# Layer 1 of a graph kernel: a third edge group per turn picked by column copies, the turned one-hot in straight order, and the steps of the engines re-ordered

## What is computed

```python
e_in = jnp.concatenate([x[src], x[dst]], axis=-1)
edge_new = relu(e_in @ We1 + be1) @ We2 + be2
agg = segment_sum(edge_new, dst, num_segments=N)
mesh_new = relu(concatenate([x, agg]) @ Wn1 + bn1) @ Wn2 + bn2
x = layernorm(x + (x + mesh_new))
```

## Time and profile before

| | |
|---|---|
| runs | 4099.94, 4093.49, 4094.84 us; median 4094.84 |
| profiled execution, its own time | 4090.99 us |
| its span (first to last instruction) | 4088.8 us |
| granted TensorE clock, mean | 0.844 of full |
| busy share of the span | PE 71%, weight loads 65%, DVE 61%, ACT 61%, POOL 73% |
| layer 1's edge loop, first gather to end of last | 2179.3 to 4060.6 us |

### The profile page before, as it was taken

How to read it: one execution, slowest core, us unless ns; L and a number is a source line. 1 busy time by engine, 2 the same in 40 slices (tenths; PEclk the granted TensorE clock), 3 DMA queues, 4 the chain that set the end, 5 groups by cost and what they waited for, 6 DMA issues and landing times. The chain is left out here.

```text
span 4088.8 us, 90253 instructions
## 1 busy us (share of the span) xinstructions
PE 2902.8 (71%) x18890; PEld 2648.6 (65%) x18891; DVE 2493.5 (61%) x5568; ACT 2497.4 (61%) x10068; POOL 2964.7 (73%) x3137
## 2 busy tenths in 40 slices
PE   6888888888888788888865565655556565666656
PEld 4877777777777777777744555555556555555656
DVE  4877777777777777777765444444444555555544
ACT  3767777777777677777646555455555555555553
POOL 5777777777777777777536777777777777777775
PEclk8999999999999999999987777767767777777777
DMA  6333333333333333333234333333333333333332
GB/s 190 81 81 81 83 81 81 81 82 81 82 80 82 81 84 81 81 81 83 57 108 108 95 90 94 94 91 94 90 94 94 93 99 94 98 97 95 97 99 63
DMA packets 426429, 367.97 MB, mean 90 GB/s; under 512 B 276875, under 2 KB 355163, under 8 KB 426108
## 3 DMA queue, kind: packets, MB, share of 16 engines
q0 software_dynamic: 98240, 214.20, 20.4%
q1 hardware_dynamic: 316720, 143.31, 14.0%
q10 hardware_dynamic: 11214, 8.17, 0.7%
HBM read 343.89 MB, written 21.44 MB: 89 GB/s over the span
## 5 line engine op out<-in xcount | busy, mean ns | idle before, releaser
L724 POOL DMA_INDIRECT he<-h_table,src_i x1563 | 1480.7, 947 | 514.9 <-issue 504.3
L1744 POOL DMA_INDIRECT msg<-p_table,src x1507 | 1422.3, 944 | 467.1 <-issue 461.6
L1777 PE MATMUL p_sumT<-msg,hot 128*80 128x129 f32 x3136 | 595.7, 369 | 688.2 <-ACT sumT L1830 683.7
L1777 PEld LDWEIGHTS p_sumT<-msg,hot 128*80 128x80 f32 x3136 | 542.5, 215 | 725.4 <-issue 533.9
L1622 ACT COPY picked<-hT 128x1 f32 x7168 | 759.9, 187 | 412.4 <-issue 398.3
L1762 PE MATMUL p_edge<-r_win,hotT 80*128 80x128 f32 x3136 | 480.0, 312 | 59.7 <-DVE msg L1899 45.8
L763 PE MATMUL p_score<-qk_two,heT 128*128 128x160 f32 x1568 | 396.7, 336 | 165.4 <-ACT heT L873 163.4
L1762 PEld LDWEIGHTS p_edge<-r_win,hotT 80*128 80x128 f32 x3136 | 452.6, 227 | 63.7 <-issue 63.2
L1899 DVE TENSOR_TENSOR msg<-msg,p_edge 128x512 f32<-128x512 f32 x392 | 243.6, 662 | 377.5 <-DMA msg<-p_table,src 376.4
L765 PE MATMUL p_score<-qk_win,heT 128*128 128x80 f32 x3136 | 465.2, 273 | 0.0
L765 PEld LDWEIGHTS p_score<-qk_win,heT 128*128 128x128 f32 x3136 | 454.3, 200 | 0.0
(11 more groups left out here) (210 smaller groups left out, 4565.5 us busy)
## 6 DMA issues: line engine op xcount, KB each, us to landing
dst_row<-in_dst_dram SPq DMA_DIRECT2D x196, 320.0 KB
feat<-in_edge_attr_dram SPq DMA_DIRECT2D x196, 128.0 KB
he<-h_table,src_i POOLq DMA_INDIRECT x1563
msg<-p_table,src POOLq DMA_INDIRECT x1507
qk_win<-qk_table SPq DMA_DIRECT2D x196, 40.0 KB
qk_two<-qk_table SPq DMA_DIRECT2D x392, 20.0 KB
r_win<-r_table SPq DMA_DIRECT2D x196, 40.0 KB
qk_table<-qk SPq DMA_DIRECT2D x13, 512.0 KB
```

What stands on the lines that cost most here:

```text
L724: e.indirect_dma_start(out=he[u][:, j, 2 * FE:2 * FE + ROW], out_offset=None, in_=h_table[:, :], in_offset=bass.IndirectOffsetOnAxis(ap=sr ...
L1744: e.indirect_dma_start(out=msg[u][:, j, 0:D], out_offset=None, in_=p_table[:, :], in_offset=bass.IndirectOffsetOnAxis(ap=src_i[u][:, j:j + ...
L1777: mm = e.matmul(p_sumT[:, :], hot_of(c)[:, j, :], msg[u][:, j, 0:D + 1], start=(j == 0), stop=(j == J - 1))
```

## The change

Layer 1 only. Slots 5, 0 and 3 now have a picked group. The one of slot 5 is picked in every turn, those of slots 0 and 3 from turn 1 on (`group_of`). ACT copies the columns for slots 5 and 3, DVE (with `tensor_copy`) those for slot 0. DVE does so in parts of 24 columns a step (the sixth part is 8, the seventh step has none), ACT in parts of 40. `hotT` is one flat row in the order of `dst_row`, written by one instruction, and PE reads the weights of a group from it with a step of 8 numbers (7 for the seven gathered groups of a picked chunk, 1 for the picked group and for the last chunk). The steps change to: PE edges(c+1), turn_back(c-1), sums(c); ACT copy_sums(c-1), relus(c), picks; DVE hots(c+1), add(c-2), picks, boths(c). SP's loads of the picks' numbers move to other steps.

```diff
-PICKED = (5, 1)
-BY_ACT = P // BATCH
+PICKED = (5, 0, 3)
+BY_ACT = (P, 0, P)
+BY_DVE = tuple(P - n for n in BY_ACT)
...
-            hotTs = [sb(f"hotT{k}", [W, J, P], ctx=ctx) for k in range(2)]
+            hotTs = [sb(f"hotT{k}", [W, CH], ctx=ctx) for k in range(2)]
...
+            def made(of, g, turn):
+                each = sum(n > 0 for n in of)
+                upto = sum(n > 0 for n in of[0:g + 1])
+                return turn * each + (upto + each if g == 0 else upto)
...
-                        return PICKED.index(c[1]) if at_first and c[1] in PICKED else None
+                        g = PICKED.index(c[1]) if at_first and c[1] in PICKED else None
+                        return None if g and isinstance(c[0], int) and c[0] == 0 else g
...
                     def pick_step(e, engine, copy, done, c, of):
-                        per = -(-len(PICKED) * of // SLOTS)
-                        at, end = c[1] * per, min((c[1] + 1) * per, len(PICKED) * of)
+                        per = -(-sum(of) // (BATCH * (SLOTS if of is BY_ACT else SLOTS - 1))) * BATCH
+                        at, end = c[1] * per, min((c[1] + 1) * per, sum(of))
+                        for g in range(len(of)):
+                            low = sum(of[0:g])
+                            first, n = max(at - low, 0), min(end - low, of[g]) - max(at - low, 0)
                             turn = c[0] if g == 0 else c[0] + 1
+                            if n > 0 and not (isinstance(turn, int) and turn == TURNS):
+                                pick_columns(e, engine, copy, done, g, turn, first, n, of)
...
                         def load_picks(g, turn):
                             if not isinstance(turn, int) or turn > 0:
-                                before = val(e, pick_number(g, turn) - len(PICKED) + 1)
-                                e.wait_ge(picked_act, before)
+                                for done, of in ((picked_act, BY_ACT), (picked_dve, BY_DVE)):
+                                    if of[g]:
+                                        e.wait_ge(done, val(e, made(of, g, turn - 1)))
...
                         def load_picks_ahead(c):
-                            if u == 2 and not (isinstance(i, int) and i == 0):
+                            if u == 0 and not (isinstance(i, int) and i == 0):
+                                load_picks(2, i)
+                            elif u == 3 and not (isinstance(i, int) and i == 0):
                                 load_picks(0, i)
-                            elif u == 5 and not (isinstance(i, int) and i == TURNS - 1):
+                            elif u == 4 and not (isinstance(i, int) and i == TURNS - 1):
                                 load_picks(1, i + 1)
...
+                        def column(c, j):
+                            flat = hotT_of(c)
+                            if is_last(c):
+                                return flat[:, j * P:(j + 1) * P]
+                            if group_of(c) is None:
+                                return flat[:, :].rearrange("w (p j) -> w j p", j=J)[:, j, :]
+                            if j == 0:
+                                return flat[:, 0:P]
+                            return flat[:, P:CH].rearrange("w (p j) -> w j p", j=J - 1)[:, j - 1, :]
...
-                                    mm = e.matmul(p_edge[h][:, j % 4, :], hotT_of(c)[:, j, :], r_win[u][:, :], ...)
+                                    mm = e.matmul(p_edge[h][:, j % 4, :], column(c, j), r_win[u][:, :], ...)
...
                         def step(c):                      # PE
-                            if not is_first(c):
-                                sums(shift(c, -1))
-                            if not is_first(c) and not is_first(shift(c, -1)):
-                                turn_back(shift(c, -2))
                             if not is_last(c):
                                 edges(shift(c, 1))
+                            if not is_first(c):
+                                turn_back(shift(c, -1))
+                            sums(c)
...
-                        def step(c):                      # ACT
+                        def step(c, k=None):
+                            if not is_first(c):
+                                copy_sums(shift(c, -1))
+                            relus(c)
+                            if k is not None and c[1] == 4:
+                                relu_hidden(e, k)
                             if at_first:
                                 pick_step(e, mybir.EngineType.Activation, e.copy, picked_act, c, BY_ACT)
-                            if not is_first(c) and not is_first(shift(c, -1)):
-                                copy_sums(shift(c, -2))
-                            relus(c)
...
-                            row_j = "w (j p) -> w j p" if is_last(c) else "w (p j) -> w j p"
-                            j0 = 0 if group_of(c) is None else 1
-                            if j0:
-                                e.scalar_tensor_tensor(out=hotT_of(c)[:, 0, :], in0=dst_row[u][:, 0:P], ...)
-                            e.scalar_tensor_tensor(out=hotT_of(c)[:, j0:J, :], in0=dst_row[u][:, j0 * P:CH].rearrange(row_j, j=J - j0), ...)
+                            e.scalar_tensor_tensor(out=hotT_of(c)[:, :], in0=dst_row[u][:, :], scalar=start_b[0:W, bass.ds(number(c), 1)],
+                                                   in1=p_node.broadcast_to([W, CH]), op0=ALU.subtract, op1=ALU.is_equal).then_inc(hotT_done, 1)
...
                         def step(c):                      # DVE
                             if not is_last(c):
                                 hots(shift(c, 1))
-                            boths(c)
                             if not is_first(c) and not is_first(shift(c, -1)):
                                 add(shift(c, -2))
+                            if at_first:
+                                pick_step(e, mybir.EngineType.DVE, e.tensor_copy, picked_dve, c, BY_DVE)
+                            boths(c)
```

More of the change, by code:

```diff
@@ L1615, in pick_columns @@
                                 e.sem_inc(passed, 1)
-                        for b in range(first, first + n):
-                            at = b * BATCH
+                        start = first + (0 if of is BY_ACT else BY_ACT[g])
+                        for at in range(start, start + n, BATCH):
                             _, nodes = nc.values_load_multi_w_load_instructions(
@@ L1622, in pick_columns @@
                                 op = copy(picked[g][:, at + k:at + k + 1], x1T[:, bass.ds(nodes[k], 1)])
-                        if first + n == of:
+                        if first + n == of[g]:
                             op.then_inc(done, 1)
                     def pick_step(e, engine, copy, done, c, of):
-                        per = -(-len(PICKED) * of // SLOTS)
-                        at, end = c[1] * per, min((c[1] + 1) * per, len(PICKED) * of)
-                        while at < end:
-                            g = at // of
-                            n = min(end, (g + 1) * of) - at
-                            turn = c[0] if g == 0 else c[0] + 1
[L1634 to L1639, removed]
+                        per = -(-sum(of) // (BATCH * (SLOTS if of is BY_ACT else SLOTS - 1))) * BATCH
[3 more added lines that the diff above has]
+                            first, n = max(at - low, 0), min(end - low, of[g]) - max(at - low, 0)
+                            turn = c[0] if g == 0 else c[0] + 1
+                            if n > 0 and not (isinstance(turn, int) and turn == TURNS):
+                                pick_columns(e, engine, copy, done, g, turn, first, n, of)
                     @block.sync
@@ L1713, in _ @@
                         if at_first:
-                            for g in (1, 0):
-                                load_picks(g, 0)
+                            load_picks(0, 0)
                         for u in range(1, SLOTS):
@@ L1761, in edges @@
                                 for j in range(4 * h, 4 * h + 4):
-                                    mm = e.matmul(p_edge[h][:, j % 4, :], hotT_of(c)[:, j, :], r_win[u][:, :], start=True, stop=(j > 0 or g is None))
+                                    mm = e.matmul(p_edge[h][:, j % 4, :], column(c, j), r_win[u][:, :], start=True, stop=(j > 0 or g is None))
                                     if j == 0 and g is not None:
-                                        ready = val(e, pick_number(g, c[0]) + 1)
-                                        e.wait_ge(picked_act, ready)
+                                        for done, of in ((picked_act, BY_ACT), (picked_dve, BY_DVE)):
+                                            if of[g]:
+                                                e.wait_ge(done, val(e, made(of, g, c[0])))
                                         mm = e.matmul(p_edge[0][:, 0, :], picked[g][:, :], we1[:, 0, :], start=False, stop=True)
@@ L1830, in copy_sums @@
```

(15 more changed lines are left out.)

26 lines of the change are left out of this document (10 added, 16 removed).

## The result

| | before | after |
|---|---|---|
| median of the runs | 4093.81 us (8 runs) | 4108.18 us (8 runs) |
| profiled execution: span | 4088.8 us | 4107.1 us |
| granted TensorE clock, mean | 0.844 | 0.827 |

The ratio is 1.0034, 95% interval 1.0023 to 1.0045: slower by 0.3%. Faster was forecast, 4061.4 us with a range up to 4096. The chain that ended last and its shares by line (page of after) say who sets the time now; before, the same line began with POOL 30% and issue 12%.

A forecast was written before the change was run, and what follows sets the result against it. POOL's full gather queue was taken as the bound. From 4090.99 us, 32.4 for fewer gathers and 1.0 at the end gave 4057.6; with 3.85 from that execution to the median of the runs, 4061.4, range 4052 to 4096.

The forecast's parts named there:

- the loop through PE and DVE: Layer 1, boths through edges, turning back, add and copies: 59.0 and 62.6 us a turn, under POOL's 66.1.
- Copies: DVE's column copies, 128 a turn: 0.162 us each by ACT's all-in figure, 20.7 us a turn (12.2 to 31.1).
- Edges: PE's edges of a chunk: 3.20 us at the low clock, plus 0.5 us for stepped weights.
- The load itself: PE's weight load of 128 columns read with a step: 0.23 us each, 16 of them 3.7 us.
- B: DVE's column copies cost more, at 0.20 us loops of 63.9 and 67.5 us and 4081 us in all; chance 8%.
- A: PE's stepped weights add to the low clock level, 1.55 us more a chunk, slower at 4120 us; chance 11%.
- C: DVE's copies hold up POOL's gathers by 0.095 us each, 328 us in all, 4390 us; chance 3%.
- D: Late boths(i, 0) makes POOL wait for sums about 1.2 us a turn, time stays near 4093; chance 4%.
- the forecast 6.6 us: DVE's wait once a turn for the numbers of the picks, in its step (i, 0): some 6.6 us.
- Some 40 us away: Distance from late boths(i, 0) to POOL's gather waiting for sums 7 chunks back, so the lateness costs no time.
- the 32.4 us: POOL's saving in layer 1: 26 gathers fewer at 1.248 us each.
- the 1.0 us taken: Gain at the end of the span from sums(c) following boths(c) in the same step, at best 2.3 us.

The follow-up runs named there:

- run 1: The changed kernel with DVE's column copies and add moved behind boths(c); 4058.45 us, ratio 0.9908 to the kernel before.
- run 8: The kernel before with flat hotT and PE's weights read with a step, orders and picks as before; 4140.94 us, ratio 1.01.
- run 4: The changed kernel with two picked groups (slots 5 and 3), both on ACT, no column copies on DVE; 4096.66 us, ratio 1.0001 to the kernel before.
- run 2: The changed kernel with hotT written group by group again, so PE reads its weights in order; 4063.48 us, ratio 0.9916 to the kernel before.
- run 6: The changed kernel with DVE's copies ahead of add(c-2), both still ahead of boths(c); 4067.78 us, ratio 0.9927 to the kernel before.
- run 10: The kernel before with flat hotT, stepped weights and PE's step as edges, sums, turn_back; 4438.47 us, ratio 1.0827.

## Why the prediction was wrong

**The step that failed** is the sum of the loop through PE and DVE: "59.0 and 62.6 us" against POOL's 66.1. The loop was the right one, and it was checked against the right bound; it measured 66.99 and 69.07. Two of its terms were too small and one link was left out. By kind of step, for turns 2 to 13:

- Copies: 0.162 us each was taken, from ACT. A batch of 8 on DVE follows the last by 1.55 us (2913.54 to 2915.09) and a part has an entry of 0.43 us: 24 copies are 4.78 us, 0.199 each. That is 4.7 us a turn, and the largest part. The prediction had both signs of this in its bounds (0.095 to 0.243) and took the other engine's figure.
- Edges: 3.70 us was taken for a chunk, 3.97 measured, 4.20 with a picked group (2916.83 to 2921.03). That is 2 to 3 us a turn. The load itself was priced well: from one to the next it is 0.238 us where 0.23 was taken. The rest is the start and the end of the row of loads and, in a picked chunk, the two products with `we1`.
- A link that was left out: there are two `hotT` buffers and seven slots, so slots 6 and 0 share one, and `hotT` of slot 0 waits until the edges of slot 6 are done. The timeline of after at that slot:

```profile
2924.73 3.89 PE L1779 MATMUL p_edge<-r_win,hotT 80*128 80x128 f32 x16
...
2928.66 1.28 DVE L1894 SCALAR_TENSOR_TENSOR hotT<-dst_row,start_b,p_iota 80x1024 f32<-80x1024 int32 x1 [2.79 <-PE p_edge L1779]
```

The step without copies lasts 6.69 us, not 5.47. Five steps of 24 columns at 10.60 in the mean (9.36 predicted), one of 8 at 7.30 (6.77) and this one at 6.69 (5.47) make 67.0 where 59.0 was forecast. In the later turns it was 6.5 us above.

Against 66.1 the excess is 13 x 0.9 + 13 x 3.0 = 51 us for turns 1 to 26. The account above finds 16.9 + 28.7 = 45.6 of it.

**Once a turn** DVE also stands before `in_win`, 24 times and 61.6 us in all, with nothing waited for that the profile shows, up to 4.3 us:

```profile
3410.69 1.12 DVE L1574 TENSOR_SCALAR o_last<-y_last,mv_last,rstd_last 128x128 f32<-128x128 f32 x4
3414.38 0.23 DVE L1887 TENSOR_SCALAR in_win<-dst,start_b 128x8 f32<-128x8 int32 x1 [2.57 <-issue]
```

Before, only 7 such gaps showed at the add, 18.4 us, and DVE's time was in any case covered by its waits for landings. It stands where the loop's body begins again, and the packets of the instruction queue rose from 230 to 367. The other runs go the same way: those in which DVE copies columns have 295 to 368 packets and 33.8 to 68.6 us of these gaps, those in which it copies none have 228 to 231 packets and at most 4.9 us. Loading of code would fit, but no run tests it. In run 1 such gaps are as large, 63.1 us, and cost nothing.

**The rivals.** B (dear copies) is the nearest: its price of 0.20 is what was measured, its loop of 63.9 and 67.5 us lacks the other terms, and its 4081 is 27 us short. A (the step on top of the low clock) had the sign right and the mechanism wrong: on top of the clock's own pace, a load would take 0.31 us at a granted clock of 0.50 and 0.21 at 1.00 (0.213 and 0.112 in order, plus 0.097), and it takes 0.23 to 0.24 at both. It is a limit, as the prediction took it, and of the size worked out. The sign named for A, loads of 0.3 us, would have misled: the records of L1779 last 0.326 us in the mean, but each begins before the one ahead of it has ended. C is refuted: the gathers' mean is 944 ns, as before, beside 3,456 DVE copies. The trap of the Trainium skill, "SBUF — State Buffer", section "SBUF: two separate sides", does not show at these one-element copies. D's waits came (20.5 us on sums), and fit a lag built up over many turns better than a late slot 0: no gap before the copies is as long as the forecast 6.6 us.

**"Some 40 us away"** was right about a single delay and wrong about a rate. A loop that is 1 to 3 us a turn too long uses up any distance: it ended as POOL's waits and as a tail longer by 28.7 us. The margin to be checked was that of the loop, with each link priced on its own engine.

**Right:** 1,481 gathers at 944 ns, 1.27 us for each `hotT`, 3,456 copies, no loss through SP or ACT. And the 32.4 us: run 1 gets them, at 4058.45 us where 4061.4 was forecast, with one line of the order changed. The end was won by more than the 1.0 us taken: from the last gather's end to the span's end run 1 takes 26.2 us, against 28.2 before.

## What to carry to other kernels

When work is moved under a wait, write the loop down that closes through that engine, from an instruction round to itself, and place the new work outside it: the same 128 copies cost about 50 us between the add and boths and nothing behind boths. Price an instruction on the engine that will run it; a margin of one tenth does not cover another engine's figure. And an order that hides a slow link in one kernel is part of the price of every edit: the stepped weights cost 1% in the old order (run 8), nothing in the new one while DVE copies nothing (run 4), and about 1.2% in the new one with the copies in the loop (after against run 2).

## What the runs showed of the hardware

**Weight loads with a step.** The windows of after over 14 stepped loads, over the 16 in-order loads of the last chunk (both with a few neighbours at their ends in counts and busy times), and over 16 stepped loads; columns as in the earlier trace rows, the granted clock third from the end:

```profile
4071.80:4075.20 3.40, 3.40 (x19) 3.40 (x19) 0.18 (x1) 0.37 (x1) 0.00 (x0) 1.00 0.00 0
4077.80:4079.80 2.00, 2.00 (x21) 2.00 (x21) 1.47 (x5) 0.75 (x1) 0.00 (x0) 1.00 0.00 0
2906.20:2910.20 4.00, 3.96 (x16) 3.99 (x17) 2.75 (x4) 2.61 (x17) 3.09 (x4) 0.50 0.41 116
```

The loads of the first two windows in the timeline, 16 in-order loads of run 2 at a granted clock of 0.50, and the group on the page of after:

```profile
4071.72 3.30 PEld L1779 LDWEIGHTS p_edge<-r_win,hotT 80*128 80x128 f32 x14
...
4077.74 1.87 PEld L1779 LDWEIGHTS p_edge<-r_win,hotT 80*128 80x128 f32 x16
...
2923.58 3.48 PEld L1780 LDWEIGHTS p_edge<-r_win,hotT 80*128 80x128 f32 x16 [8.99 <-DVE msg L1915]
...
L1779 PEld LDWEIGHTS p_edge<-r_win,hotT 80*128 80x128 f32 x3136 | 745.0, 326 | 468.0 <-issue 318.9
```

The pace is the time from one load's start to the next one's, that is the length of a row less its last record, over the loads but one. In order it is 0.213 us at a clock of 0.50 (1.2 GHz) and 0.112 at 1.00 (2.4 GHz). With a step of 7 f32 it is 0.23 us at both (0.229 in the first row here), with a step of 8 it is 0.24 (0.238 over the 16 loads from 2906.21; the median over layer 1 is 0.240 at the low clock and 0.238 at the high one). So the step costs a tenth at the low clock and doubles the time at the high one, and with it a higher clock brings the edges nothing. The mean granted clock was 0.827 against 0.844 before; across the runs it does not follow PE's busy share (0.844 at 79% in run 6, 0.797 at 74% in run 10). The Trainium skill, "SBUF — State Buffer", section "Door 1: The DMA port swizzle", says that such reads pay a penalty. The trace agrees and gives its size, for PE as above and for DVE (2.045 us for `hotT` with a step of 8, 1.271 in order).

**A 128 x 1 copy with its column from a register.** On DVE a copy lasts 154 ns, one follows the next in a batch after about 0.115, and the loading of the next 8 registers leaves 0.59 us of nothing: 0.199 us all-in, against 0.162 on ACT, whose copy lasts longer (187 ns) but whose gap is 0.47.
